# A graph layer on one core: 256 table rows for two more tiles, fetched one by one by ScalarE

## The reference

```python
h = maximum(layernorm(x), 0);  s, v = h[:, :64], h[:, 64:].reshape(n, 32, 3)
xs, xv = s @ W1_s / 8, einsum('nmc,mk->nkc', v, W1_v) / sqrt(32)     # the table
w = silu(edge_embed @ fc_w1 + fc_b1) @ fc_w2 + fc_b2                 # 192 weights per edge
xs_e, xv_e = xs[src], xv[src]                                        # the gather
m0_a = w_ss * xs_e * sh0;   m1_a = (w_sv * xs_e) x sh1
m1_b = w_vs * xv_e * sh0;   m0_b = w_vv * sum_c(xv_e * sh1) / sqrt(3)
agg = segment_sum(concat(m0_a, m0_b, m1_a, m1_b), dst) / sqrt(0.5)
out = agg @ W2 + h @ Wsc, gated;   return x + h + feats
```

## Time and profile before

| | us |
|---|---|
| median of 3 runs | 536.1 (535.06 to 536.38) |
| the profiled execution | 535.7 |
| its span, first to last instruction | 534.0 |
| TensorE busy / VectorE / ScalarE / GpSimd | 470.2 / 353.6 / 200.3 / 392.0 |
| mean granted TensorE clock | 0.952 of full |

### The profile page before, as it was taken

How to read it: one execution, slowest core, us unless ns; L and a number is a source line. 1 busy time by engine, 2 the same in 40 slices (tenths; PEclk the granted TensorE clock), 3 DMA queues, 4 the chain that set the end, 5 groups by cost and what they waited for, 6 DMA issues and landing times.

```text
span 534.0 us, 17321 instructions
## 1 busy us (share of the span) xinstructions
PE 470.2 (88%) x5423; PEld 348.3 (65%) x5423; DVE 353.6 (66%) x1236; ACT 200.3 (38%) x445; POOL 392.0 (73%) x421
## 2 busy tenths in 40 slices
PE   6968898897999988988898898889889889999996
PEld 6935566575677756666665666666567666767675
DVE  8856765566567666666767656676665666766766
ACT  5964233332333333334333333333334332444341
POOL 6757777777777777777777777777777777777772
PEclk9987789899599999999999999999999997999898
DMA  9972222222222222222222222222222322222221
GB/s 195 352 209 74 71 70 74 71 74 76 73 72 69 78 76 68 78 74 77 72 72 77 72 73 78 78 69 76 77 69 75 79 75 70 78 74 76 72 69 44
DMA packets 36089, 46.15 MB, mean 86 GB/s; under 512 B 10312, under 2 KB 28971, under 8 KB 35795
## 3 DMA queue, kind: packets, MB, share of 16 engines
q0 software_dynamic: 19776, 33.78, 23.5%
q1 hardware_dynamic: 15865, 11.90, 8.1%
q10 hardware_dynamic: 410, 0.07, 0.1%
HBM read 39.61 MB, written 4.00 MB: 82 GB/s over the span
## 4 chain that ended last, share of the span: by engine, by line
POOL 34%; PE 23%; issue 19%; DMA 11%; SPq 6%; DVE 4%; DVEq 2%; ACT 0%; POOLq 0%
POOL gath L607 34%; DMA gath<-table,src_sb 10%; PE ps L951 7%; PE ps L961 5%; PE ps L938 3%; PE ps L956 3%; DVE P L739 3%; SPq L212 3%; PE ps L944 1%; PE ps L943 1%; SPq L194 1%; PE ps L957 1%; DVEq L781 1%; SPq L208 1%; DMA table<-prod 1%
## 5 line engine op out<-in xcount | busy, mean ns | idle before, releaser
L607 POOL DMA_INDIRECT gath<-table,src_sb x388 | 367.6, 948 | 122.1 <-issue 110.3
L961 PE MATMUL ps<-S,P 128*64 128x24 f32 x2496 | 169.5, 220 | 0.0
L951 PE MATMUL ps<-fc_sb,hid 128*128 128x384 f32 x416 | 162.6, 516 | 2.6 <-ACT ps L673 2.6
L956 PE MATMUL ps<-S,P 128*64 128x36 f32 x832 | 119.0, 237 | 48.3 <-DVE P L739 45.9
L961 PEld LDWEIGHTS ps<-S,P 128*64 128x64 f32 x2496 | 158.5, 141 | 0.0
L956 PEld LDWEIGHTS ps<-S,P 128*64 128x64 f32 x832 | 82.1, 139 | 113.5 <-issue 91.3
L653 ACT ACTIVATE hid<-ps,fb_sb 128x256 f32<-128x256 f32 x104 | 49.2, 473 | 218.0 <-PE ps L938 130.1
L734 DVE TENSOR_TENSOR P<-ps,gath 128x512 f32<-128x512 f32 x102 | 70.5, 691 | 86.4 <-DMA gath<-table,src_sb 78.0
L673 ACT COPY ps<-fb_sb 128x768 f32<-128x768 f32 x104 | 83.5, 803 | 91.3 <-DVE P L739 91.2
L957 PE MATMUL ps<-S,P 128*64 128x12 f32 x832 | 108.7, 208 | 0.0
L796 DVE TENSOR_TENSOR agg<-ps,agg 128x48 f32 x412 | 84.7, 206 | 29.5 <-DVE agg L796 4.5
(11 more groups left out here) (122 smaller groups left out, 341.6 us busy)
## 6 DMA issues: line engine op xcount, KB each, us to landing
slow<-table SPq DMA_DIRECT2D x512, 0.6 KB
gath<-table,src_sb POOLq DMA_INDIRECT x388, 2.6
agg<-zeros SPq DMA_DIRECT2D x2, 1024.0 KB, 15.0
out<-res SPq DMA_DIRECT2D x24, 78.1 KB
x_sb<-x SPq DMA_DIRECT2D x5, 350.0 KB
emb<-emb_t SPq DMA_DIRECT2D x104, 16.0 KB
table<-prod SPq DMA_DIRECT2D x3, 420.0 KB
sh_sb<-sh_t SPq DMA_DIRECT2D x1, 840.0 KB
```

The lines of the kernel that those rows point to most:

```text
L607: nc.gpsimd.indirect_dma_start(gath[:, u, j, :], None, table, bass.IndirectOffsetOnAxis(ap=src_sb[:, t:t + 1], axis=0)).then_inc(arrived, 16)
L951: ins = nc.tensor.matmul(w_ps(u)[:, 2 * g:2 * g + 2, 0:WN], hid[:, u % 2, g, :], fc2_sb[:, :, :], start=False, stop=True, skip_group_check ...
L956: nc.tensor.matmul(oj[0:64, 0:3, :], pj[:, 64:128], sj[:, 1:4, :], start=True, stop=True)
L961: ins = nc.tensor.matmul(oj[64:128, c:4:3 - c, :], pj[:, lo:lo + 64], sj[:, 0:2 + c:1 + c, :], start=(c == 0), stop=(c == NC - 1), skip_gr ...
```

## The change

NS goes from 4 to 6, so the slow tiles are those of rounds 20 to 25 and GpSimd's gathers become 386. SyncE fetches the tiles of rounds 20, 21, 22 and 25 (512 rows as before, 11 per two steps). ScalarE fetches those of rounds 23 and 24: 256 rows, 6 per two steps, three behind each step's other work, from group 4 to group 89, with a register load of six indices in every second step. ScalarE's loop is written out over all 26 rounds, and it copies two tiles more from `slow` to `gath`. VectorE's loop ends at round 20 instead of 22.

```diff
-NS, ROWS = 4, 11
+NS, ROWS, ACT_ROWS = 6, 11, 6
+SP_TILES, ACT_TILES = (0, 1, 2, 5), (3, 4)
 SLOW_FROM = NI - NS
+SP_ROWS = len(SP_TILES) * TE
...
-            for m in range(NS):
+            for k, m in enumerate(SP_TILES + ACT_TILES):
                 t = (SLOW_FROM + m) * SLOTS * QT + 2 * QT - 1
-                sp.dma_start(slow_i[:, m * TE:m * TE + TE], src_q[t:t + 1, :]).then_inc(s_slow, 16)
+                sp.dma_start(slow_i[:, k * TE:k * TE + TE], src_q[t:t + 1, :]).then_inc(s_slow, 16)
...
-                            m, p = (n0 + k) // TE, (n0 + k) % TE
+                            m, p = SP_TILES[(n0 + k) // TE], (n0 + k) % TE
                             sp.dma_start(slow[p:p + 1, m, :], table[bass.ds(r, 1), :]).then_inc(p_slow[m], 16)
...
+                    def indices(n0):
+                        n1 = min(n0 + ACT_ROWS, NS * TE - SP_ROWS)
+                        return nc.values_load_multi_w_load_instructions(
+                            slow_i[0:1, SP_ROWS + n0:SP_ROWS + n1], engines=[mybir.EngineType.Activation], min_val=0,
+                            max_val=N - 1, skip_runtime_bounds_check_because="src lies in [0, N)")[1]
+
+                    def rows(n0, idx):
+                        for k, r in enumerate(idx):
+                            m, p = ACT_TILES[(n0 + k) // TE], (n0 + k) % TE
+                            act.dma_start(slow[p:p + 1, m, :], table[bass.ds(r, 1), :]).then_inc(p_slow[m], 16)
...
-                    for i in range(LEAD + 1):
+                    for i in range(NI):
+                        if i == 1:
+                            act.wait_ge(s_slow, 16 * NS)
+                            act.wait_ge(s_tabw, TABLE_IN)
                         for u in range(SLOTS):
                             step(i, u, i - LEAD if i >= LEAD else None)
+                            n0 = ACT_ROWS * ((i * SLOTS + u - SLOTS) // 2)
+                            if 0 <= n0 < NS * TE - SP_ROWS:
+                                if u % 2 == 0:
+                                    idx = indices(n0)
+                                    rows(n0, idx[0:ACT_ROWS // 2])
+                                else:
+                                    rows(n0 + ACT_ROWS // 2, idx[ACT_ROWS // 2:])
...
-                    with act.Fori(LEAD + 1, SLOW_FROM) as i:
-                        for u in range(SLOTS):
-                            step(i, u, i - LEAD)
-                    for i in range(SLOW_FROM, NI):
-                        for u in range(SLOTS):
-                            step(i, u, i - LEAD)
```

More of the change, by code:

```diff
@@ L52 @@
 assert NR % RG == 0
+SP_ROWS = len(SP_TILES) * TE
+assert len(SP_TILES + ACT_TILES) == NS
 assert NI * SLOTS == NQ and NN * NTN == N and NG * G == NN and NI - LEAD == NN - 2
@@ L557, in indices @@
                     def indices(n0):
-                        n1 = min(n0 + ROWS, NS * TE)
+                        n1 = min(n0 + ROWS, SP_ROWS)
                         return nc.values_load_multi_w_load_instructions(
@@ L575, in _ @@
                             n0 = ROWS * ((i * SLOTS + u - SLOTS) // 2)
-                            if 0 <= n0 < NS * TE:
+                            if 0 <= n0 < SP_ROWS:
                                 if u % 2 == 0:
```

## The result

The changed kernel takes 533.16 us in the median of four runs (531.6 to 533.59) beside 536.24 of the kernel before (535.06 to 536.61). The ratio is 0.9953, 95% interval 0.9931 to 0.9975: 2.5 us less (1.3 to 3.7); the two medians alone are 3.1 us apart. Forecast were 533.6 us and a ratio of 0.9953. That the ratio agrees to the fourth digit is luck: the interval is 1.2 us wide to either side.

The account below looks back on a forecast made before the run. GpSimd's back-to-back gathers, 1.25 us each, were taken to bound the kernel. Two gathers less save 2.5 us, all other parts cost 0: 536.1 - 2.5 = 533.6 us, range 532.5 to 537.0.

Parts of the forecast that it names:

- GpSimd sets the pace, 1.25 us a gather: GpSimd's gathers from 37.48 on: it all but never stops, 387 steps of 1.25 are 484 us.
- The sum's one term, 2 x 1.25: Two gathers less on GpSimd, in rounds 20 and 21: 2.5 us gained, bounds 0 and 2.5.
- The others follow in rounds 20 and 21: Other engines keep up with 14-gather rounds of 17.5 us; spare 5 to 6 us before round 20, about 4.5 behind.
- still gaining: TensorE in an earlier 14-gather round (468.8 to 486.4): busy 17.15 of 17.60 us, yet said to be gaining.
- rival 4: Rounds 20 and 21: TensorE at its lower clock needs over 17.5 us, all 2.5 lost, 536.1 us; chance 0.03.
- 256 rows on ScalarE cost nothing: ScalarE's issues and loads, 8.0 us a round beside 6.74 busy, fit into 18.75 or 17.5; cost 0.
- L653 was to come 0.3 late: ScalarE's activation in slot 0, behind one load and three row issues (2.65 us in a 2.36 us space).
- Rival 1: ScalarE up to 2 us late each round, GpSimd pauses take back the gain: 535.0 to 537.0 us; chance 0.20.
- Rival 2: ScalarE's rows and loads exceed the round, 19.4 us against 18.75: 543 us, or much more without overlap; chance 0.11.
- The bound of 0.84 a row: Upper price of a row issue on ScalarE: 0.664 us from its late issue plus 0.18 around it; 0.45 was taken.
- Rival 3: ScalarE's issues hold up SyncE's through a shared descriptor block; emb late, near 577 us; chance 0.04.
- The loop written out: ScalarE's loop over all rounds: removes a branch per round and adds code; cost 0.

Follow-up runs that it names:

- gathers only: Changed kernel with its two gathers less but ScalarE's loop as before and no row issues on ScalarE; 535.55 us, ratio 0.9973 to the kernel before.
- The moved list: Changed kernel with ScalarE's row numbers moved by two values (8 bytes) in their tile; 815.33 us in one run, on a chip where the kernel before took 813.8.
- ten-tile kernel: Changed kernel with ten slow tiles, six fetched by ScalarE (768 rows), 382 gathers; 611.75 us, ratio 1.1428 to the kernel before.

## Why the prediction was right, step by step

- *GpSimd sets the pace, 1.25 us a gather.* Shown from both sides: two, four and 17 gathers less give 2.5 (or 1.5 in the kernel with nothing else), 4.6 and 19.8 us, each with 2.5, 5.0 and 21.25 inside its interval, while neither ScalarE's loop nor its rows change anything that the intervals can tell. The sum's one term, 2 x 1.25, is what the timeline shows (2.50 of the 2.85 between first and last gather).
- *The others follow in rounds 20 and 21.* The spare is 5.6 and 4.3 us behind, as forecast. The prediction's words that TensorE is "still gaining" in a round of 14 don't fit: the spare falls by about 1 us, then stays. With fourteen gathers in 21 of the rounds GpSimd paused twice, for 0.5 us in all, so rival 4 was out for two rounds at this clock, but the margin is small: 16.35 of 17.5 us at the full clock.
- *256 rows on ScalarE cost nothing.* The row was sized 0.45 and is 0.37; the load 1.3 and is 0.93 or 1.52; per round 8.0 was forecast and it is 12 x 0.37 + 0.5 + 2.45 = 7.4. L653 was to come 0.3 late and came 0.03 late. That the cost is 0 to the last tenth isn't shown: the bound is 0.8 us.
- *Rival 1 (pauses)* did not come about in the profiled run. The clock fell in this run too (0.50 in the window below, columns as in the earlier trace rows), and the chain that ended last shows the weights of group 30 with it; GpSimd's timeline has the gather of group 32:

```profile
184.00:186.00 2.00, 2.00 (x4) 0.67 (x2) 1.35 (x7) 1.33 (x5) 1.68 (x2) 0.50 0.28 77
```
```profile
183.76 2.56 PE ps L969 x4
```
```profile
189.01 0.95 POOL L610 DMA_INDIRECT gath<-table,src_sb  x1 [0.30 <-issue]
```

  186.32 for a gather at 189.01: 2.7 us left, no pause. Its cause, a ScalarE late by 2 us, wasn't there (0.03). Pauses as such come without it: 1.02 of idle time in the kernel before, 2.39 in gathers only.
- *Rival 2 (ScalarE the bound)* is real, but needs between two and three times the rows: not at 24 a round, well over at 36 and 48. Its sum had the overlap wrong (5.3 of the 6.5 busy us run beside the queue, not 3.2) and left out the queue's waits of 3.1; the two errors nearly cancel. The bound of 0.84 a row, from an issue of 13 rows beside SyncE's, was the wrong neighbour.
- *Rival 3 (SyncE held up)* left no mark: 0.228 an issue in both kernels. The Trainium skill's shared and locked descriptor block (Perfetto Trace Analysis, DMA Instruction — HWDGE) can't be seen here. In the changed kernel's trace 111 of ScalarE's issues run while one of SyncE's does and 102 don't (the first behind each load left out): 0.217 in the median for both, 0.219 and 0.218 in the mean. SyncE's 105 that meet one of ScalarE's take 0.228, like its 407 others. ScalarE's longest, 0.538, is one of the 43 first issues behind a load, which take 0.45 to 0.54.
- *The loop written out* costs and brings nothing that could be measured (between 0.9 us gained and 1.8 lost).

## What to carry to other kernels

Where an engine runs the same instruction back to back from start to end, its count times its period sets the time, whatever the busy shares of the others say; take instructions off it, and read from the spare of the others how many. An engine with idle time in each step can take over the issuing of small DMAs, as long as issues and register loads, added to the waits that hold its queue, fit into the round: here 11.3 of 17.5 us did and 19.6 didn't, and what lies between wasn't measured. Size both from a row of that engine; the upper bounds taken from other places, 0.84 and 2.89, were twice what came. Load index lists into registers from starts that are a multiple of four values of the list, in counts that are a multiple of four. Of the versions that gather the right rows, the best one timed on an ordinary chip has eight slow tiles with 12 values per load (ratio 0.9914).

## What the runs showed of the hardware that I had not expected

- The time of a load of values from SBUF into registers depends on where it starts in the list. On a multiple of four values: 6 values 0.93 us, 12 0.96, 16 1.19, 18 1.64 (ScalarE), 11 values 1.73, 12 0.96 (SyncE). Off it: 6 values 1.52 us and 18 values 4.05 (ScalarE), 11 values 2.46 or 2.88 (SyncE). The moved list shows the start as the cause for the six; that the count should be a multiple of four too is read from 11 beside 12, in kernels on different chips, and wasn't tested by itself.
- Issues and loads of ScalarE's queue run beside its own compute: 5.3 of 6.5 busy us a round in the ten-tile kernel.
- The first DMA issue behind such a load takes 0.45 us on ScalarE, the next ones 0.22.
- Where TensorE had to wait for ScalarE in every round, its mean granted clock was lower: 0.864 in the ten-tile kernel, beside 0.949 in the one with fourteen gathers and 0.93 to 0.97 in the kernel before, on the same chip. Two windows of ten tiles, one round each, with the clock behind the busy times:

```profile
300.20:322.00 21.80, 19.73 (x219) 15.07 (x217) 12.42 (x42) 6.01 (x13) 14.48 (x16) 0.84 0.26 65
322.00:343.90 21.90, 18.91 (x194) 13.70 (x192) 12.35 (x42) 5.75 (x16) 14.13 (x16) 0.85 0.26 65
```

  Whether the lower clock adds to the time of these rounds isn't shown.
- Chips differ: twice a chip granted TensorE about 0.74 and took 812 us for the kernel that takes 536 elsewhere, with TensorE's matmuls in front of 47 to 53 of GpSimd's gathers. The clock isn't shown to be all of it: there the first gather of the table, too, starts only at 58.76 us (ten tiles), not at 37.48.
